# A DLRM tower with a compressed interaction network: eight running sums on VectorE, six groups of products on ScalarE, the whole first layer in three fp32r passes

## What is computed

```python
e = stack([tbl_f[ids[:, f]] for f in range(39)], axis=1)         # (512, 39, 16)
Xi = X0 = e
for W, b in ((W0, b0), (W1, b1), (W2, b2)):                      # W: (128, 39 * fields of Xi)
    Xi = einsum('hjk,bjd,bkd->bhd', W.reshape(H, 39, -1), X0, Xi) + b[None, :, None]
    res.append(Xi.sum(axis=2))
z = concatenate(res, axis=1)
h = maximum(concatenate([z, dense_ctx], axis=1) @ W_top1 + b_top1, 0)
h = maximum(h @ W_top2 + b_top2, 0)
y = h @ W_top3                                                   # (512, 1)
```

## Time and profile before

| | us |
|---|---|
| median of 3 runs | 688.73 (688.02 to 689.34) |
| the profiled execution | 685.9 |
| its span, first to last instruction | 684.0 |
| TensorE (PE) busy | 641.0 |
| its weight loads (PEld) busy | 507.6 |
| VectorE (DVE) busy | 558.1 |
| ScalarE (ACT) busy | 441.3 |
| GpSimd (POOL) busy | 464.6 |

### The profile page before, as it was taken

The page is one execution under the profiler, slowest core; times in us unless marked ns, Lnnn a source line. Parts: engine busy times, 40 slices in busy tenths (PEclk is TensorE's granted clock), DMA queues, the critical chain, the costliest instruction groups (busy, mean ns, idle before and its releaser), DMA issues.

```text
span 684.0 us, 10984 instructions
## 1 busy us (share of the span) xinstructions
PE 641.0 (94%) x2920; PEld 507.6 (74%) x2920; DVE 558.1 (82%) x1560; ACT 441.3 (65%) x1434; POOL 464.6 (68%) x372
## 2 busy tenths in 40 slices
PE   0069999999999999999999999999999999999997
PEld 0037777777778877777788877877778887777877
DVE  4149999999994599999995589999997489999860
ACT  4026877777773477777684477778685377777751
POOL 6746888888874478787886368787886377444440
PEclk9999999999999999999999999999999999999988
DMA  6146424031312102213131200403040300300000
GB/s 217 41 128 242 149 67 122 11 109 24 97 36 80 52 3 56 79 35 99 27 107 27 95 13 18 115 19 115 18 117 16 102 17 14 117 2 5 1 1 1
DMA packets 39057, 44.35 MB, mean 65 GB/s; under 512 B 17427, under 2 KB 22253, under 8 KB 38867
## 3 DMA queue, kind: packets, MB, share of 16 engines
q1 hardware_dynamic: 33363, 42.34, 20.3%
q0 software_dynamic: 5632, 1.31, 2.1%
HBM read 8.86 MB, written 0.00 MB: 13 GB/s over the span
## 4 chain that ended last, share of the span: by engine, by line
PE 92%; DMA 2%; POOL 2%; SPq 1%; ACT 1%; issue 1%; DVE 1%; DVEq 0%
PE p_u L606 22%; PE p_u L608 21%; PE p_u L607 21%; PE p_tower L625 6%; PE p_x L583 6%; PE p_g L616 5%; PE p_x L580 2%; PE p_x L577 2%; PE p_x L578 2%; POOL emb L277 2%; PE p_tower L652 1%; DMA fac_b<-xx 1%; PE p_tower L638 1%; PE p_tower L637 1%; PE p_x L562 1%
## 5 line engine op out<-in xcount | busy, mean ns | idle before, releaser
L362 ACT ACTIVATE prod<-p_u,x0t 128x128 f32<-128x128 f32 x1024 | 289.3, 375 | 91.3 <-PE p_u L608 91.0
L496 DVE SCALAR_TENSOR_TENSOR parts<-p_u,x0t,parts 128x128 f32<-128x128 f32 x1024 | 283.0, 339 | 41.5 <-PE p_u L608 41.5
L606 PE MATMUL p_u<-w1h,x1h 128*128 128x512 f32 (+1 forms) x640 | 286.6, 448 | 2.3 <-DVE x1l L473 2.3
L608 PE MATMUL p_u<-w1h,x1l 128*128 128x512 f32 (+1 forms) x640 | 250.2, 391 | 0.0
L607 PE MATMUL p_u<-w1l,x1h 128*128 128x512 f32 (+1 forms) x640 | 249.9, 390 | 0.0
L277 POOL DMA_INDIRECT emb<-table_in,idx_all x176 | 204.5, 1162 | 51.4 <-issue 47.8
L296 POOL TENSOR_TENSOR parts<-parts,prod 128x512 f32<-128x512 f32 x128 | 176.3, 1378 | 57.8 <-ACT prod L362 44.2
L606 PEld LDWEIGHTS p_u<-w1h,x1h 128*128 128x128 f32 x640 | 121.0, 189 | 38.4 <-issue 9.7
L607 PEld LDWEIGHTS p_u<-w1l,x1h 128*128 128x128 f32 x640 | 121.6, 190 | 35.4 <-issue 10.1
L291 POOL TENSOR_TENSOR parts<-prod 128x512 f32<-128x512 f32 x64 | 83.6, 1306 | 86.8 <-ACT prod L362 86.1
L608 PEld LDWEIGHTS p_u<-w1h,x1l 128*128 128x128 f32 x640 | 120.6, 188 | 26.1
(11 more groups left out here) (56 smaller groups left out, 346.9 us busy)
## 6 DMA issues: line engine op xcount, KB each, us to landing
fac_b<-xx SPq DMA_DIRECT2D x96, 234.0 KB
fac_a<-xx SPq DMA_DIRECT2D x48, 78.0 KB
emb<-table_in,idx_all POOLq DMA_INDIRECT x176, 2.8
g_all<-w_in SPq DMA_DIRECT2D x3, 832.0 KB, 9.6
xx<-xx SPq DMA_DIRECT2D x32, 78.0 KB
fac_b<-xx SPq DMA_DIRECT2D x16, 156.0 KB
w<-w_in SPq DMA_DIRECT2D x1, 2496.0 KB, 10.2
bd<-x0t SPq DMA_DIRECT2D x128, 10.0 KB
```

What stands on the lines that cost most here:

```text
L362: last = nc.scalar.activation(dst[:, i * H:(i + 1) * H], u[:, i * H:(i + 1) * H], ACT.Copy, scale=x0t[:, par, t, j:j + 1])
L496: nc.vector.scalar_tensor_tensor(out=chain[i][:, p], in0=u[:, i * H:(i + 1) * H], scalar=x0t[:, par, t, j:j + 1], in1=add, op0=ALU.mult, o ...
L606: nc.tensor.matmul(u, xh, wh, start=True, stop=False)
L608: nc.tensor.matmul(u, xl, wh, start=False, stop=True).then_inc(u_full, 1)
```

## The change

- All seven first-layer groups go in three fp32r passes: three more high halves on ScalarE, three more low halves on VectorE a macro. The rings of two stay, and their waits are adapted. TensorE no longer reads the unsplit `w0`, which now lies in `z0` and is used only until it has been split; VectorE waits for that before its first product.
- ScalarE takes six quads of a tile, q = 0, 2, 4, 5, 7, 9, VectorE four, q = 1, 3, 6, 8.
- VectorE keeps eight running sums. Its first quad starts four of them (with b1 and the three products of q = 0), its second quad the other four (with the four products of q = 2, which go to `start` as well). Both quads wait for ScalarE. The third and fourth add to the sums.
- GpSimd adds the products of q = 4, 5, 7 and 9, and its waits move accordingly.
- The fold sums 12 x 128 columns and moves from q = 7 to q = 5 of the next tile.

```diff
-SPLIT = (0, 2, 4, 6)
+SPLIT = tuple(range(GROUPS))
-Q_X2 = 7
+Q_X2 = 5
-CHAIN_TILE = 20
-A_TILE = 5
+ACT_QUADS = (0, 2, 4, 5, 7, 9)
+DVE_QUADS = (1, 3, 6, 8)
+STARTS = 7
+SUMS = 8
+CHAIN_TILE = 4 * len(DVE_QUADS)
+A_TILE = len(ACT_QUADS)
...
-        w0 = sb("w0", [ROWS, GROUPS * H])
...
+        w0 = z0[:].rearrange("p r c -> p (r c)")[:, 0:GROUPS * H]
...
-        start = sb("start", [128, 2, 3, H])
+        start = sb("start", [128, 2, STARTS, H])
-        parts = sb("parts", [128, 2, 4, H, 2])
-        chain = [parts[:, :, i // 2, :, i % 2] for i in range(4)]
-        prod_sum = parts[:, :, 2:4].rearrange("p t a h i -> p t a i h")
+        parts = sb("parts", [128, 2, (SUMS + 4) // 2, H, 2])
+        chain = [parts[:, :, i // 2, :, i % 2] for i in range(SUMS)]
+        prod_sum = parts[:, :, SUMS // 2:].rearrange("p t a h i -> p t a i h")
...
             elif M > 0:
-                engine.wait_ge(l0_added, GROUPS * (M - 1) + SPLIT[i - HALVES_RING] + 1)
+                engine.wait_ge(l0_added, GROUPS * (M - 1) + max(range(i, GROUPS, HALVES_RING)) + 1)
...
-                    pool.wait_ge(a_scaled, A_TILE * T + 3)
+                    pool.wait_ge(a_scaled, A_TILE * T + 4)
...
-                        pool.wait_ge(a_scaled, A_TILE * T + 2 + i)
+                        pool.wait_ge(a_scaled, A_TILE * T + 3 + i)
...
                 act.wait_ge(u_full, QUADS * T + q + 1)
-                if q == 0:
+                a = ACT_QUADS.index(q)
+                if a == 0:
                     need(act, chained, CHAIN_TILE * (T - 2) + 4)
-                    dst = start[:, p].rearrange("p a h -> p (a h)")
+                    dst = start[:, p, 0:3].rearrange("p a h -> p (a h)")
+                elif a == 1:
+                    need(act, chained, CHAIN_TILE * (T - 2) + 8)
+                    dst = start[:, p, 3:7].rearrange("p a h -> p (a h)")
                 else:
                     need(act, summed, SUM_TILE * (T - 2) + 3)
-                    dst = prod[:, p, q // 2 - 1, :]
+                    dst = prod[:, p, a - 2, :]
...
-                        if q % 2 == 0:
+                        if q in ACT_QUADS:
                             scale_quad(T, tt, q)
...
-                k = q // 2
+                k = DVE_QUADS.index(q)
                 dve.wait_ge(u_full, QUADS * T + q + 1)
+                if k < 2:
+                    dve.wait_ge(a_scaled, A_TILE * T + k + 1)
                 if k == 0:
-                    dve.wait_ge(a_scaled, A_TILE * T + 1)
                     need(dve, x2_made, T - 1)
                 u = p_u[(QUADS * tt + q) % RING]
                 for i, j in enumerate(QUAD_J[q]):
-                    if k == 0:
-                        add = b1[:] if i == 0 else start[:, p, i - 1, :]
+                    c = 4 * (k % 2) + i
+                    if k < 2:
+                        add = b1[:] if c == 0 else start[:, p, c - 1, :]
                     else:
-                        add = chain[i][:, p]
-                        dve.wait_ge(chained, CHAIN_TILE * T + 4 * (k - 1) + i + 1)
+                        add = chain[c][:, p]
+                        dve.wait_ge(chained, CHAIN_TILE * T + c + 1)
                     nc.vector.scalar_tensor_tensor(
-                        out=chain[i][:, p], in0=u[:, i * H:(i + 1) * H], scalar=x0t[:, par, t, j:j + 1],
+                        out=chain[c][:, p], in0=u[:, i * H:(i + 1) * H], scalar=x0t[:, par, t, j:j + 1],
                         in1=add, op0=ALU.mult, op1=ALU.add).then_inc(chained, 1)
...
-                        if q % 2 == 1:
+                        if q in DVE_QUADS:
                             chain_quad(T, tt, q)
...
+            dve.wait_ge(w0l_made, 1)
             for k in range(GROUPS):
                 product(0, 0, 0, k)
...
-                if k in SPLIT:
-                    i = SPLIT.index(k)
-                    zh, zl = z0h[0:rows, i % HALVES_RING, :], z0l[0:rows, i % HALVES_RING, :]
-                    pe.wait_ge(z0h_made, len(SPLIT) * M + i + 1)
...
-                else:
-                    pe.wait_ge(z0_made, GROUPS * M + k + 1)
-                    nc.tensor.matmul(p_x1[:], w0[0:rows, h], z0[0:rows, k % Z_RING, :],
-                                     start=first, stop=final).then_inc(l0_added, 1)
+                zh, zl = z0h[0:rows, k % HALVES_RING, :], z0l[0:rows, k % HALVES_RING, :]
+                pe.wait_ge(z0h_made, GROUPS * M + k + 1)
+                nc.tensor.matmul(p_x1[:], w0h[0:rows, h], zh, start=first, stop=False)
+                nc.tensor.matmul(p_x1[:], w0l[0:rows, h], zh, start=False, stop=False)
+                pe.wait_ge(z0l_made, GROUPS * M + k + 1)
+                nc.tensor.matmul(p_x1[:], w0h[0:rows, h], zl, start=False, stop=final).then_inc(l0_added, 1)
...
-                if q0 % 2 == 0:
-                    pe.wait_ge(a_scaled, A_TILE * T0 + q0 // 2 + 1)
+                if q0 in ACT_QUADS:
+                    pe.wait_ge(a_scaled, A_TILE * T0 + ACT_QUADS.index(q0) + 1)
                 else:
-                    pe.wait_ge(chained, CHAIN_TILE * T0 + 4 * (q0 // 2 + 1))
+                    pe.wait_ge(chained, CHAIN_TILE * T0 + 4 * (DVE_QUADS.index(q0) + 1))
```

## The result

| | before | after |
|---|---|---|
| median of 4 runs (us) | 688.41 | 727.97 |
| the profiled execution's span (us) | 684.0 | 724.6 |

The ratio is 1.0577, 95% interval 1.0554 to 1.0600: the changed kernel is 5.8% slower. The sign was forecast, the size was not: the forecast was 712, the range ended at 722. The 40.5 us between the two spans (724.56 less 684.05 to the hundredth) are the subject of the rest.

A forecast was written before the change was run, and what follows sets the result against it. PE bounds the kernel before; after the change DVE with ACT does, at 37.17 us a macro. Macros +19.5, prologue +3.2 and end +0.8 sum to +23.5 us, added to the 688.7 median: 712 us, range 698 to 722.

The forecast's parts named there:

- prologue: Before the macros: three more split groups in series, less a transfer wait already there, +3.2 us, all on the path.
- macro 0: First macro: starts empty and has no fold in its first tile, -0.3 us.
- macros 1, 2, 3, 6, 7, 10, 11, 14: Macros that start with the backlog: +1.95 us each, 15.6 us in all.
- macros 5, 9, 13: Macros after a tower: one quad's 1.04 us of room spent first, an estimate; 3 x 0.9 = 2.7 us.
- macros 4, 8, 12 (tower): Macros holding a tower: stall 0.5 to 1.0 us before tower work, gain 0.48; +1.5 us in all, an estimate.
- PE's saving: Groups 1, 3 and 5 in three passes: 0.70 instead of 0.86 us each, 0.48 us a macro, allowing 34.74 us.
- The forced waits: DVE waits for ACT's products before quads 3, 11, 21 and 31: 0.76, 0.34, 1.56, 0.95; 3.61 us a macro.
- DVE's bare work: DVE's work a macro: 33.79 + 1.80 (low halves) - 4.16 (quads) + 2.13 (fold) = 33.56 us, nearly unchanged.
- A rule weighed: GpSimd's adds delaying DVE's low halves and products: at worst 0.97 us more an instruction, taken as nothing.
- PE stays the bound: Rival, chance 0.12: ACT's halves and quads fit into DVE's gaps, -3.2 us, 685.5 us.
- half the waits: Rival, chance 0.14: DVE's waits partly coincide with waits for PE, +1.0 a backlogged macro, +14.4 in all, 703 us.
- Low halves held up: Rival, chance 0.05: GpSimd's adds delay each new low half, 2.9 us a macro, 744 us at most, half of it 728.

The follow-up runs named there:

- Quad-first with small adds: Changed kernel with ScalarE taking its quad before the high half and GpSimd's adds cut to one column in 128: 684.16 us, ratio 0.9991.
- small adds: Changed kernel with GpSimd's adds cut to one column in 128, waits and order unchanged: 704.97 us, ratio 1.0242.
- quad-first kernel: Changed kernel with ScalarE taking its quad before the high half in each slot: 720.9 us, ratio 1.0471.
- the kernel without the second wait: Changed kernel with VectorE's second quad not waiting for ScalarE's quad 2, whose products are left out: 721.85 us, ratio 1.0565.
- the one with eight sums alone: Kernel before with eight sums, six quads on ScalarE and the longer fold, but four split groups as before: 721.31 us, ratio 1.0485.

## Why the prediction was right or wrong

The 40.5 us between the spans, stage by stage (starts of z1; the last row is from the z1 of macro 15 to the end of the span):

| stage | forecast | measured |
|---|---|---|
| prologue | +3.2 | +5.6 |
| macro 0 | -0.3 | +1.4 |
| macros 1, 2, 3, 6, 7, 10, 11, 14 | +15.6 | +23.8 |
| macros 5, 9, 13 | +2.7 | +10.1 |
| macros 4, 8, 12 (tower) | +1.5 | -0.7 |
| macro 15 and end | +0.8 | +0.3 |
| sum | +23.5 | +40.5 |

**The bound, right.** DVE's cycle with ACT took the place of PE, and PE waits for low halves. Quad-first with small adds, which removes DVE's hold-ups and about half of its waits and nothing of PE's or ACT's work, brings PE back to 38.02 of 38.20 us. PE's saving was priced right too: from the start of the group to the start of the second pass behind it, an fp32 group takes 1.10 us (287.95 to 289.05, before) and three passes 0.94 (287.26 to 288.20, both changes in one kernel), 0.16 less, three times a macro. But no run has a macro of 34.7 us.

**The forced waits, right.** 3.08 us a macro against 3.61, with three of four places within 0.15 us. The fourth was hidden behind a hold-up: with small adds it is back at 0.32 us and the sum is 3.50.

**DVE's bare work, right.** With small adds DVE is busy 33.16 us in a macro of 36.65 (290.43 to 327.08), against the 33.56 forecast, which had some 0.5 us of hold-ups of before in it. The fold of 1536 took 1.745 us against 1.74. The forecast of 37.2 us a macro is in effect one of the changed kernel without hold-ups (36.7).

**The step that failed: "A rule weighed".** The forecast priced GpSimd's hold-ups at nothing, from the low halves' rows of before (669 to 780 ns), and left them a rival with a chance of 0.05. The same rows had a product of 1649, and the step read it as an exception. It was not, and the product of 1.05 us that the forecast used for quads 20 and 21 was held up too. Hold-ups were a matter of where an instruction falls between adds. In the kernel before, 34 of the 96 long products started during an add, and none of the 48 long low halves did. In the changed kernel 55 of 96 and 27 of 96 did. With the new order 96 long products averaged 829 ns and 96 low halves 773, by the groups' means 1.8 us of hold-ups a macro against 0.8 before, and 1.6 us of work above the forecast in the plain macro read above. Over the kernel that is 26 us of hold-ups against 11, and the forecast was 17 short. The Trainium skill, "SBUF — State Buffer", "Who interferes with whom", has this rule: a VectorE instruction with two SBUF inputs contends with a GpSimd instruction that reads SBUF, and the one that comes second is blocked until the other ends. These traces agree: DVE's instructions end 0.55 us after the add's end, and with small adds none is longer than 693 ns. It holds the other way as well: in the quad-first kernel 12 adds began some 0.2 us after a low half, which took its 0.68 us, and each of these adds took 1.63 to 1.66 us instead of 1.31. By the rule the low halves' rows should not have overruled the product's. Two rows do not fit it: the products of 339.40 and 322.20 started 0.64 and 0.63 us ahead of the add and were still the ones that stood, while a third in the same place, at 338.82 in the kernel without the second wait, took 0.67 us. Why is open.

**Macros 5, 9 and 13: the room was not there.** I let 1.04 us be spent first, an estimate without a row. These macros took 38.6 us, 3.4 more than before. Part of this may be a shift, since the tower macro ahead ends with the same z1. Taken as pairs, macros 4 to 5, 8 to 9 and 12 to 13 cost 2.1, 3.5 and 3.8 us, against 1.4 each in the forecast. Macro 4 came off best because it had been slow before: 53.2 us at a granted clock of 0.97, against 51.8 and 51.6 us for macros 8 and 12 at 1.00. After, all three take 52.0 us at 1.00. That is luck in the row of the towers.

**Macro 0** was taken as bound by PE. DVE waited 1.44 us before quad 3 in it, the forced wait again.

**Prologue.** The three more groups in series came as forecast (a split group goes from product to product in 1.99 us). On top, the high half of group 5 started 1.45 us after its product had ended:

```profile
45.70 0.69 DVE L466 TENSOR_TENSOR z<-fac_b,fac_a 117x512 f32<-117x512 f32 x1
...
47.84 0.63 ACT L335 ACTIVATE z0h<-z 117x512 fp32r<-117x512 f32 x1 [2.78 <-PE p_x L589]
```

What held ACT up isn't shown. Such a gap stands at another place in the kernel with small adds (group 6) and in the one with eight sums alone, and is missing in quad-first with small adds, so it varies from kernel to kernel or run to run. It stays open.

**Rivals.** "PE stays the bound" and "half the waits" fell. "Low halves held up" was the right mechanism at some 1 to 1.6 us a macro, a third to a half of its price of 2.9, and it added to the forced waits instead of being a case apart: products were held up too, which the rival left out. That its half price names 728 us, the measured time, is luck.

**The scale of a measurement.** The kernel before took 688.4 to 688.8 us in two sessions and 684.7 in a third, so kernels of different sessions are best compared by ratio.

## What to carry to other kernels

When two engines run at 96 and 100%, write out the in-order cycle of the second one with its waits before moving work between them. Nearly equal work (33.8 and 33.6 us here) says little when an engine that was idle in the right places is now waited for: 3.1 us of forced waits left nothing of PE's saving of 0.5. And if some instructions of a kind show a maximum at twice their median, look up which instruction of the other engine ran beside each one; a new order will deal those overlaps afresh. Before removing a wait, look at what its release will run into.

## What was unexpected of the hardware

DVE's instruction with two inputs in SBUF stands still while GpSimd adds, and ends 0.55 us after it. Of 224 products and low halves in the changed kernel, 109 started in an add, and all of them keep to this. Twice one stood though it had started first, during a gather with an add right behind (2.50 us for an instruction of 0.68). Removing one wait of 0.76 us gave back nothing that four runs could tell, and two causes that are worth 7 and 23 us alone are worth 40 together.
